# Second biases of three leaf layers: gathered beside the delta rule instead of inside the leaf stage

## The reference

```python
node = jnp.zeros(x.shape[:2], dtype=jnp.int32)
for _ in range(DEPTH):                                  # DEPTH = 8
    logit = jnp.einsum('bsd,bsd->bs', x, nw[node]) + nb[node]
    node = 2 * node + 1 + (logit > 0).astype(jnp.int32)
leaf = node - NN
h = act(jnp.einsum('bsd,bsdl->bsl', x, w1[leaf]) + b1[leaf])
return jnp.einsum('bsl,bsld->bsd', h, w2[leaf]) + b2[leaf]
```

## Time and profile before

| | us |
|---|---|
| median of 3 runs | 4191.34 |
| lowest, highest | 4176.77, 4198.45 |
| span of the profiled execution, its own time as far as the page tells it | 4248.5 |
| delta stage with its routing, in the profiled execution | about 138 to 2136 |
| leaf stage of trees 0 to 2 | 2136 to 2519 |
| leaf stage of tree 3 | about 2801 to 2935 |

### The profile page before, as it was taken

How to read it: one execution, slowest core, us unless ns; L and a number is a source line. 1 busy time by engine, 2 the same in 40 slices (tenths; PEclk the granted TensorE clock), 3 DMA queues, 4 the chain that set the end, 5 groups by cost and what they waited for, 6 DMA issues and landing times. The chain is left out here.

```text
span 4248.5 us, 63196 instructions
## 1 busy us (share of the span) xinstructions
PE 3365.2 (79%) x23196; PEld 2356.3 (55%) x23196; DVE 2202.2 (52%) x4869; ACT 1752.7 (41%) x4289; POOL 836.9 (20%) x923
## 2 busy tenths in 40 slices
PE   3588887787888888887767679445569999999998
PEld 3356655565665566666656557335534555555554
DVE  5466666456677566666233345523533444544444
ACT  1466655555565555565232231022123333333331
POOL 0000011300001310001255642354300111011110
PEclk6799987788897798997587889778778999999999
DMA  4200000200000200001164623163620000000000
GB/s 136 91 16 17 21 6 16 89 17 21 17 12 30 81 16 11 21 7 35 56 214 155 191 97 108 55 219 132 232 102 13 21 26 26 11 25 16 21 16 15
DMA packets 187998, 256.17 MB, mean 60 GB/s; under 512 B 31664, under 2 KB 135728, under 8 KB 187312
## 3 DMA queue, kind: packets, MB, share of 16 engines
q1 hardware_dynamic: 152240, 180.67, 13.2%
q0 software_dynamic: 18432, 50.49, 3.3%
q10 hardware_dynamic: 17024, 20.97, 1.4%
HBM read 171.08 MB, written 81.00 MB: 59 GB/s over the span
## 5 line engine op out<-in xcount | busy, mean ns | idle before, releaser
L523 PE MATMUL banks<-s_d_xT,s_w_qkvg 128*128 128x512 f32 x640 | 355.9, 684 | 24.3 <-DMA s_d_xT<-xnT 17.8
L2452 ACT ACTIVATE s_g_pT<-banks 128x1536 f32<-128x1536 f32 (+1 forms) x96 | 152.9, 1592 | 448.8 <-PE banks L2340 448.8
L616 DVE SCALAR_TENSOR_TENSOR s_d_kq<-banks,s_conv_w,s_d_kq 128x511 f32<-128x511 f32 (+2 forms) x384 | 286.4, 747 | 48.7 <-ACT s_d_kq L568 38.3
L2416 DVE TENSOR_REDUCE s_g_nmax<-banks 128x4 f32<-128x512 f32 (+3 forms) x128 | 188.0, 1490 | 192.2 <-PE banks L2324 192.1
L839 ACT ACTIVATE s_d_X<-s_d_Xc 32x256 f32<-32x256 f32 x320 | 131.9, 412 | 278.6 <-DVE s_d_Xc L870 202.3
L2765 PE MATMUL banks<-s_m_we,s_m_tT 128*128 128x512 f32 x512 | 233.9, 602 | 3.5 <-DVE s_m_x L2828 3.2
L1684 ACT ACTIVATE s_q_hT<-banks,s_q_w 128x128 f32<-128x128 f32 x252 | 91.6, 367 | 315.2 <-PE banks L1652 213.6
L1652 PEld LDWEIGHTS banks<-s_q_xsT,s_q_w 128*128 128x128 f32 x1008 | 168.8, 213 | 69.3 <-issue 53.0
L1652 PE MATMUL banks<-s_q_xsT,s_q_w 128*128 x1008 | 173.9, 300 | 42.0 <-issue 30.3
L523 PEld LDWEIGHTS banks<-s_d_xT,s_w_qkvg 128*128 128x128 f32 x640 | 125.6, 215 | 142.4 <-issue 126.8
L1661 PE MATMUL banks<-s_q_w,s_q_hm 128*128 (+1 forms) x504 | 172.8, 428 | 36.5 <-DVE s_q_hm L1705 22.9
(11 more groups left out here) (380 smaller groups left out, 8147.8 us busy)
## 6 DMA issues: line engine op xcount, KB each, us to landing
s_q_w<-w12p SPq DMA_DIRECT2D x128, 257.0 KB
s_q_xs<-xs SPq DMA_DIRECT2D x32, 516.0 KB
s_r_xT<-xfT SPq DMA_DIRECT2D x12, 1024.0 KB
s_r_work<-xf SPq DMA_DIRECT2D x24, 512.0 KB
og<-s_d_o SPq DMA_DIRECT2D x16, 512.0 KB
s_b_og<-og SPq DMA_DIRECT2D x8, 1024.0 KB, 9.4
s_x_in<-x SPq DMA_DIRECT2D x8, 512.0 KB, 4.4
xf<-s_xf_rows SPq DMA_DIRECT2D x8, 512.0 KB, 4.0
```

Of the source, the lines that this page charges most:

```text
L523: ins = e.matmul(bk[6 + j % 2][:], w[:, par, c, self.COL[what] + h * P:self.COL[what] + (h + 1) * P], xT[:, c, :], start=(c == 0), stop=(c ...
L616: e.scalar_tensor_tensor(d[:, a:], bk[6 + j % 2][:, 0:SEQ - a], cw[:, par, k0 + 3 - a:k0 + 4 - a], d[:, a:], ALU.mult, ALU.add).then_inc(s ...
L2416: e.tensor_reduce(self.nmax[:, t, :].rearrange("p (k d) -> p k d", k=4)[:, :, 16], psum[:, 0:4, a:a + (t + 1) * P], AX.X, ALU.max, negate= ...
L2452: e.activation(self.pT[c][:], psum[:, 0:4, 0:self.COLUMNS[c]], ACT.Exp).then_inc(self.exped, 1)
```

## The change

Three edits.

1. **Trees 0 to 2: the biases are laid down before the leaf stage.** DVE writes a table `leafi` of leaf numbers in the order of the tokens, not sorted (one more instruction for each tree, so `SORT` is 44). POOL gathers 32 tiles of biases for each tree into two buffers `bias` (`gather_bias`), and SP stores each tile to its 128 plain rows of `tree0`, `tree1`, `tree2` (`store_bias`). A gather waits for the store of two tiles before it, a store for its gather. For tree F - 1 these stand beside the routing of tree F, a gather at every third step and its store two steps later. For tree 2 they follow as 32 steps of their own behind its routing. In the leaf stage DVE clears `acc` to zero in pieces of four tiles (`clear`, 128x1024, 8 for each tree, 24 in all), and the scatter adds to what lies in DRAM (`compute_op=ALU.add`) in place of overwriting it.
2. **Tree 3 keeps its gather and its plain scatter**, with two semaphores for gathers in place of four: a gather waits for the landing of the one two before it.
3. **The leaf numbers are spread in bfloat16.** DVE casts them to `leafb` and PE multiplies by a bfloat16 identity. The casts (`numbers_vector`) stand before the mask at the segment of the first turning step, where the index tables stood behind the third segment after it. `d_square`, a scrap output of ACT in the delta rule, becomes bfloat16 to make room.

```diff
-    RT, V, SORT, PLACED = 8, 23, 43, 31
+    RT, V, SORT, PLACED = 8, 23, 44, 31
...
+    def gather_bias(self, e, F, t):
+        u = TILES * F + t
+        e.wait_ge(self.sorting, self.SORT * (F + 1))
+        if u >= 2:
+            e.wait_ge(self.bias_out[u % 2], 16 * (u // 2))
+        e.indirect_dma_start(self.bias[:, u % 2, :], None, self.g.dram["b2"], bass.IndirectOffsetOnAxis(self.leafi[:, F, t:t + 1].bitcast(U32), 0)).then_inc(self.bias_in[u % 2], 16)
+
+    def store_bias(self, e, F, t):
+        u = TILES * F + t
+        e.wait_ge(self.bias_in[u % 2], 16 * (u // 2 + 1))
+        e.dma_start(self.g.dram[f"tree{F}"][ds(t * P, P), :], self.bias[:, u % 2, :]).then_inc(self.bias_out[u % 2], 16)
+
+    def biases(self, e, F, what, step):
+
+        if F > self.trees[0] and step % 3 == what and step // 3 < TILES:
+            (self.gather_bias, None, self.store_bias)[what](e, F - 1, step // 3)
...
     def steps_sync(self, e):
...
             yield from self.seats_sync(e, F)
+        for t in range(TILES):
+            self.store_bias(e, self.trees[-1], t)
+            yield
...
     def steps_gpsimd(self, e):
         for F in self.trees:
-            for _ in range(self.LEAD + 23 * self.ROUNDS):
+            for step in range(self.LEAD + 23 * self.ROUNDS):
+                self.biases(e, F, 0, step)
                 yield
             yield from self.seats_gpsimd(e, F)
+        for t in range(TILES):
+            self.gather_bias(e, self.trees[-1], t)
+            yield
...
-                ins = e.matmul(bank[:, t * P:(t + 1) * P], xs[:, t, LEAF:LEAF + 1].broadcast_to((P, P)), self.g.ident[:], start=True, stop=True)
+                ins = e.matmul(bank[:, t * P:(t + 1) * P], self.leafb[b % 2][:, t:t + 1].broadcast_to((P, P)), self.g.identb[:], start=True, stop=True)
...
+            if self.based:
+                f, b = (first, n // 4) if Q < SEGS * first + TILES else ((Q - self.CLEAR) // SEGS + 1, (Q - self.CLEAR) % SEGS // 4)
+                if first <= f <= last and b < N_BATCH and (n if f == first else Q - self.CLEAR - SEGS * (f - 1)) % 4 == 0:
+                    self.clear(e, f, b)
+            if self.beside(Q) and self.beside(Q)[2] == 0:
+                self.numbers_vector(e, *self.beside(Q)[:2])
...
-        e.indirect_dma_start(self.g.dram[f"tree{F}"], bass.IndirectOffsetOnAxis(self.toki[F % 2][:, t:t + 1].bitcast(U32), 0), self.acc[:, t * DIM:(t + 1) * DIM], None).then_inc(self.unsorted[t % 4], 16)
+        e.indirect_dma_start(self.g.dram[f"tree{F}"], bass.IndirectOffsetOnAxis(self.toki[F % 2][:, t:t + 1].bitcast(U32), 0), self.acc[:, t * DIM:(t + 1) * DIM], None, compute_op=ALU.add if self.based else ALU.bypass).then_inc(self.unsorted[t % 4], 16)
...
-            if F == first and 2 <= n < TILES + 2:
+            if not self.based and 2 <= n < TILES + 2 and F == first:
                 self.gather(e, first, n - 2)
-            ahead = Q - self.GATHER
-            if ahead >= SEGS * first and ahead // SEGS < last and ahead % SEGS < TILES:
-                self.gather(e, ahead // SEGS + 1, ahead % SEGS)
```

More of the change, by code:

```diff
@@ L1067, in sync @@
         e.wait_ge(self.og_out, 16 * self.CALLS)
+        for j in range(2):
+            e.wait_ge(self.routes.bias_out[j], 16 * len(self.routes.trees) * TILES // 2)
         e.sem_inc(g.over, 1)
@@ L1123, in __init__ @@
         self.posi = sb("posi", [P, TILES], I32)
+        self.leafi, self.bias = sb("leafi", [P, len(trees), TILES], I32), sb("bias", [P, 2, DIM]) if before is None else None
         self.logits_made = 16 * (trees[-1] + 1)
@@ L1143, in steps_sync @@
         for F in self.trees:
+            step = 0
             if F:
@@ L1323, in sort_vector @@
         e.tensor_scalar(seg[:, 1, 0:63], sgf[:, 64:127], -1.0, None, ALU.add).then_inc(me, 1)
+        e.tensor_scalar(self.leafi[:, F - self.trees[0], :], self.lf[:], float(F * LEAVES), None, ALU.add).then_inc(me, 1)
     def steps_vector(self, e):
@@ L1498, with __init__ @@
     U, LOADS, LAG = 16, 9, 2
-    COPIES, SCATTER, GATHER, AHEAD = 6, 40, 46, 3
+    COPIES, SCATTER, CLEAR, AHEAD = 6, 40, 48, 3
     ROWS_FROM, COLUMNS_FROM, WEIGHTS_FROM = 31, 36, 34
-    def __init__(self, g, trees, act, before=None):
-        self.g, self.trees, self.act = g, trees, act
+    def __init__(self, g, trees, act, routes, before=None):
+        self.g, self.trees, self.act, self.based = g, trees, act, before is None
+        self.acc_in, self.gathered = routes.bias_in, 16 * len(routes.trees) * TILES // 2
         self.n = g.stage()
@@ L1512, in __init__ @@
         self.toki, self.leafi = ([sb(f"{n}{j}", [P, TILES], I32) for j in range(2)] for n in ("toki", "leafi"))
+        self.leafb = [sb(f"leafb{j}", [P, TPB], BF16) for j in range(2)]
         self.w12 = sb("w12", [P, GROUPS, 258 + DIM])
@@ L1545, in beside, with numbers @@
         return (F, n // 4, n % 4) if first < F <= self.trees[-1] and n < 4 * N_BATCH and n % 4 < 3 else None
+    def numbers(self, u):
+        return 2 * u + max(u - 24, 0)
     def load_rows(self, e, F, b):
@@ L1551, in load_rows @@
             e.wait_ge(self.turned, 3 * (u - 1))
-            e.wait_ge(self.numbered, 2 * (u - 1))
+            e.wait_ge(self.numbered, self.numbers(u - 1))
         e.dma_start(self.xs[b % 2][:], rows(D[f"xs{F}"], b)).then_inc(self.xs_in[b % 2], 16)
@@ L1558, in columns_tensor @@
             e.wait_ge(self.xs_in[b % 2], 16 * (u // 2 + 1))
+        if step == 2:
+            e.wait_ge(self.numbered, self.numbers(u) + 2)
         if u or step == 2:
@@ L1693, in vector @@
         e.wait_ge(g.over, 5 * self.n)
+        self.numbers_vector(e, first, 0)
         self.columns_vector(e, first, 0)
@@ L1707, in vector @@
             if q >= SEGS * first:
-                if q % SEGS < TILES:
-                    u = TILES * (q // SEGS) + q % SEGS
-                    e.wait_ge(self.acc_in[u % 4], 16 * (u // 4 + 1))
+                if self.based and q % SEGS < TILES:
+                    e.wait_ge(self.cleared, 8 * (q // SEGS - first) + q % SEGS // 4 + 1)
+                elif q % SEGS < TILES:
+                    u = q % SEGS
+                    e.wait_ge(self.acc_in[u % 2], self.gathered + 16 * (u // 2 + 1))
                 row = self.acc[:, ds(at[q] * DIM, DIM)]
@@ L1719, in vector, with clear @@
         e.sem_inc(g.over, 1)
+    def clear(self, e, F, b):
+        if F > self.trees[0]:
+            for j in range(4):
+                e.wait_ge(self.unsorted[j], 16 * (8 * (F - 1) + b + 1))
+        e.memset(self.acc[:, 4 * b * DIM:4 * (b + 1) * DIM], 0.0).then_inc(self.cleared, 1)
     def scatter(self, e, F, t):
@@ L1723, in scatter @@
         if t % TPB == 0:
-            e.wait_ge(self.numbered, 2 * (8 * F + t // TPB + 1))
+            e.wait_ge(self.numbered, self.numbers(8 * F + t // TPB + 1))
         if u >= 4:
@@ L2934, in build @@
         delta = Delta(g, lambda: Routes(g, (0, 1, 2), "xf", "xfT", (5,)))
-        segments = Segments(g, (0, 1, 2), ACT.Relu)
+        segments = Segments(g, (0, 1, 2), ACT.Relu, delta.routes)
         attention = Attention(g, delta.routes)
         stages += [delta, segments, attention, Seats(g, attention.routes)]
-        stages += [Segments(g, (3,), ACT.Gelu, segments), Combine(g), SecondLayer(g)]
+        stages += [Segments(g, (3,), ACT.Gelu, delta.routes, segments), Combine(g), SecondLayer(g)]
         g.open.close()
```

38 lines of the change are left out of this document (22 added, 16 removed).

## The result

The changed kernel takes 4208.0 us (median of 20 runs, 4184.2 to 4226.0), the kernel before 4183.2 beside it (20 runs, 4175.9 to 4201.9): ratio 1.0056, 95% interval 1.0041 to 1.0071, some 24 us slower. The forecast was 4174 against 4191, with a range of 4134 to 4222: the time lies in the range, but the change went the other way. Measured twice more: 1.0089 (1.0058 to 1.0120) beside 4178 us, and 1.0015 (0.9995 to 1.0036) on a chip where the kernel before takes 4254 us. The size differs between chips, as experiments 3 and 4 tell.

The account below looks back on a forecast made before the run. No engine was full in the leaf stage; POOL's gathers and scatters set the transitions' pace. Terms -57.5 - 3 + 2 + 50 - 11 + 2 = -17.5 us took 4191.3 to 4174, range 4134 to 4222.

Parts of the forecast that it names:

- Step 2: Leaf-stage scatters of trees 0 to 2: adding costs POOL no more than a plain scatter's 0.99 us; 2 us charged for landings.
- The rival that I gave 0.17: Leaf stage: each of 96 adding scatters costs POOL 1.0 us more, 74 us in all, so 4248 us; chance 0.17.
- floor plus 0.12: Transitions: a segment's pace lies 0.12 us above POOL's floor, as 2.85 against 2.73 in the profile.
- a rival of 4203 with 0.20: Leaf stage: DMA becomes the bound, transitions stay at 2.4 us a segment, 29 us less gained, 4203 us; chance 0.20.
- Step 1: Two leaf-stage transitions lose POOL's gathers: 1.95 us a segment, 62.4 each, 57.5 us gained, plus 3 from gathers behind them.
- POOL's floor of 1.44: Transitions without gathers: POOL's own work allows no less than 2.87 us for two segments, 1.44 each.
- the upper row: Transitions: the slower of two comparison stretches, the leaf stage's first at 2.06 us a segment; 1.95 was taken near it.
- Step 3: Delta stage: 96 gathers and stores, 74 of them where POOL waits anyway (529.8 us in one wait), cost nothing.
- Step 4: Tail between delta and leaf stage: 22 gathers and stores, 4.67 us a pair, 50 us lost (28 to 60).
- Step 5: Leaf stage: bfloat16 leaf numbers gain 14 us; tree 3's gathers with two under way lose 3; 11 stay.
- the sign that I had set at 15: Tree 3: POOL standing before its gathers for more than 15 us in all would show the forecast wrong.
- Step 6: Leaf stage: DVE's 24 clears take 1.2 to 1.4 us each, mostly in idle time; 2 us charged, 31 if uncovered.

Follow-up runs that it names:

- experiments 3 and 4: Follow-ups: two waits removed from a kernel loading biases into the accumulator (0.9969); changed kernel repeated (1.0015, 1.0089), or its tail gathers put in the leaf stage (1.0053, 1.0012).
- before: The kernel without the change, run beside the others: 4183.2 us in the main measurement, 4254 us on a slower chip.
- the second profile: The unchanged kernel profiled once more on a chip where it takes 4182 us: span 4179.2 us, against 4248.5 in the first profile.
- after: The changed kernel with all three edits, against the kernel before: 4208.0 us, ratio 1.0056; its profiled span is 4224.2 us.
- after_again: The changed kernel run once more on a slower chip, against the kernel before: 4261.0 beside 4254.0 us, ratio 1.0015.
- wide_tail: The changed kernel with tree 2's biases gathered into eight tiles instead of two and stored four at a time: 4242.9 us, 0.9959 to the kernel before, slower chip.
- bf16_only: The kernel before with the third edit alone, biases left in the leaf stage: 4239.2 us, ratio 0.9965, on a chip where the kernel before takes 4258.
- plain_no_tail: The changed kernel with plain scatters in trees 0 to 2 and without tree 2's 32 bias gathers and stores: 4112.4 us, 0.9826 to the kernel before.

## Why the prediction was wrong, point by point

*Step 2, the adding scatter, is what failed.* I bounded it between 0 and 1.30 us more and took the lower end, "since the instruction carries the same 128 indices". It takes 1.57 us against 0.98, 0.59 more, and its rows keep the DMA engines longer. I charged 2 us; it is 41 in time and 51 in the profiles of the stage.

The rival that I gave 0.17 had the mechanism: POOL's issue, in full at the end of tree 2 and in part in the transitions. Its arithmetic was not right throughout. By its own rule, floor plus 0.12, a scatter that is 0.59 us dearer has a pace of 2.15 in place of 1.95: 12.8 us in the transitions and 18.9 at the end of tree 2, 32 in all. With 8 off, since the median of before is 4183 and not 4191, that is 4198; measured 4208. The 7 us that it put to the transitions at 0.3 us more are 0 by the same rule, so the gain of 17.5 is gone from some 0.44 us on, and 0.6 gives 0.4% slower than 4191, not 0.5%. Scaled in proportion (44 of 74 us) it comes to 4210, which is near the measured time by luck: the transitions with adding scatters run at 1.92 a segment, and without at 1.45.

By the Trainium skill (DMA: Bandwidth & Descriptors, Rules for kernel authors) an accumulating DMA reads its destination and writes it later. The trace agrees in kind: half as many packets again on that queue, and full engines at 248 GB/s where plain ones move 321. The bytes that it counts stay the same, so the read itself does not show. I had that rule and gave it a rival of 4203 with 0.20, with transitions at 2.4 a segment; they run at 1.92. The row that was missing is POOL's 0.59 us.

*Step 1, the transitions, was right in its difference by two errors that cancel.* With plain scatters they take 92.5 us together, not 124.8. That is 1.45 a segment, the size of POOL's floor of 1.44, which I had worked out and then left for the upper row. But POOL alone does not hold them: it is busy 34.2 of 46.5 us and idles up to 1.36 us for DVE, while PE is busy 40.2 at a granted clock of 1.00. And what they replace is 151.1 us, not 182.3, on the chips that the time was measured on: a gain of 58.6 against 57.5 forecast. The base was too long because the one profiled execution had a span 57 us over the median, and I took "the difference over unscaled". Of the 69 us by which it is longer than the second profile, 47 lie in the leaf stages, 37 of them where the change saves. That the transitions of after, with adding scatters, take the 61.5 and 60.6 us that I forecast is luck too: a pace too high by half a us a segment, and a scatter too cheap. I also missed that the first stretch loses POOL's gathers too: 64.1 to 52.9, and the third edit is about half of that (66.0 to 58.9 with it alone on the slower chip, 52.3 with all three).

*Step 3* held on the 4180 us chips: 0 in time. On SP and POOL the gathers do wait, 67.8 us in 24 pieces before 2123, out of POOL's spare time:

```profile
POOL s_d_o L1016 <- DVE s_d_o L974: 467.3, 12, 47.0
...
POOL s_r_bias L1150 <- DMA tree<-s_r_bias: 67.8, 24, 4.8
```

That answers to the earlier trace rows, 529.8. On the slower chips after_again has a delta stage of 2024.7 us and wide_tail, which has the 64 pairs as well, 2008.4, where bf16_only without them has 1995.7: 29 and 13 us over. Whether that is the 64 pairs or the scatter between executions stays open.

*Step 4, the tail:* 50 forecast, 57.6 in the profile, 54 in time; the form (22 gathers, pairs, two landings) is as written. The pair is 0.66 us longer than the two landings that I took. By the Trainium skill (DMA: Bandwidth & Descriptors, Anatomy of one DMA), which gives about 2.0 us plus the bytes at 436 GB/s for DMAs issued from GpSimd, a 128 KB DMA is an estimated 2.3 us, and with the same for SP's store the tail is 53. The trace does not lie on that line: 2.8 for GpSimd's gather, 1.8 for SP's store, though their sum comes out the same.

*Step 5, bfloat16:* 14 forecast, 15 measured alone, on the slower chip (0.9965). The spread's products of after, by tile (ns min, median, max):

```profile
L1606 PE MATMUL banks<-c_identb,s_q_leafb x128: 216/219/314, 2189.3 to 2853.9; 128*128 128x128 bf16 x128
```

One product lasts 0.22 us in place of 0.31, but products overlap. All 128 are busy 13.0 us, 0.10 each where the float32 ones had 0.32: as forecast, and below the 0.15 that I named. Tree 3's gathers were taken at 3: POOL stands 23.3 us before them for the landing of an earlier one (the sign that I had set at 15), where it stood 22.2 for DVE's index tables before, and tree 3's stage is 3.8 us longer where the third edit alone makes it shorter by 5.8 (131.2 to 125.4, on the slower chip), so 6 to 10.

*Step 6, the clears:* 0.91 us each, below the estimate of 1.2; whether their 22 us are hidden wasn't tested by itself.

*The sum by what was measured:* tail +54, adding +41, the rest (transitions with plain scatters, first stretch, third edit, tree 3) the 0.9826 of plain_no_tail, -68 to -73: together 22 to 27, measured 24. Each term is a difference of the same chain of kernels, so the sum has to close and proves nothing by that. Set beside the forecast's terms it says where the error sits: the tail within 4 us, adding 39 us off, the rest -68 to -73 where the forecast had -69.5.

## What to carry to other kernels

Before an indirect DMA is given an operation, price it by itself: here it cost the issuing engine 60% more and the DMA engines about half as much again for the same bytes. Work that is moved "beside" another stage is free only while it fits: the 22 of 96 gathers that stuck out past its end cost 54 us. The number of buffers, not the instruction count, set their pace. And when the one profiled execution lies well off the median, profile the kernel again before a difference is worked out of its longest stretches.

## What the runs showed of the hardware that was not expected

- An indirect DMA with an add: 1.57 us on POOL against 0.98, 5.7 us to landing against 4.1 in the same stage, 27648 packets on the queue against 18432 for the same 50.49 MB, and a POOL copy started beside it takes 1.01 us in place of 0.41.
- The same kernel takes about 4180 us on three chips and 4255 on two others, with one set of runs on each chip. Of the 69 us between two profiles of it (that the first comes from a slower chip is inferred) 37 lie in the leaf stage of trees 0 to 2, 20 in the delta stage and 10 in tree 3's; after, whose transitions have full DMA engines, has the same leaf stage (319.2, 317.8, 319.6) on either.
- PE's granted clock in the same two transitions, as a share of 2.4 GHz: 0.75 and 0.79 in the first profile of before, 0.86 and 0.86 in the second, 0.94 and 1.00 in after, 1.00 and 1.00 with plain scatters. What the clock is worth there was not measured: in after POOL sets the pace.
